# One of sixteen score blocks of a head pair copied by ScalarE and folded on GpSimd; context products in two halves of columns

## The reference

```python
attn = jnp.einsum('bhqd,bhkd->bhqk', q, k) * scale
attn = jax.nn.softmax(attn.astype(jnp.float32), axis=-1)
ctx  = jnp.einsum('bhqk,bhkd->bhqd', attn, v)
```

## Time and profile before

| what | value |
|---|---|
| runs | 3328.68 us median of 3 (3327.36 to 3344.76) |
| profiled execution | 3326.78 us, its span 3325.0 us |
| TensorE, VectorE, ScalarE, GpSimd busy | 80%, 74%, 55%, 30% of the span |
| mean granted clock of TensorE | 0.908 |
| maxima of the cuts, VectorE L708 | 1024 instructions, 1204.8 us, mean 1219 ns |
| Exp, ScalarE L693 | 2048 instructions, 1064.6 us, mean 602 ns |
| context, TensorE L632 | 4096 instructions, 547.2 us |
| scores, TensorE L645 and L619 | 2048 each, 622.6 and 526.4 us |
| GpSimd waiting for the pair's maximum (L541) | 914.6 us |

### The profile page before, as it was taken

The page is one execution under the profiler, slowest core; times in us unless marked ns, Lnnn a source line. Parts: engine busy times, 40 slices in busy tenths (PEclk is TensorE's granted clock), DMA queues, the critical chain, the costliest instruction groups (busy, mean ns, idle before and its releaser), DMA issues. The chain is left out here.

```text
span 3325.0 us, 42836 instructions
## 1 busy us (share of the span) xinstructions
PE 2664.8 (80%) x12693; PEld 959.3 (29%) x12693; DVE 2465.1 (74%) x2953; ACT 1815.3 (55%) x3157; POOL 1006.7 (30%) x1271
## 2 busy tenths in 40 slices
PE   6799999985578689999998419677777777997776
PEld 3122222222256312222221218322232232332222
DVE  6999999964245499999994532679999975447468
ACT  3488888883133358888888105355555531224423
POOL 4222222210555322222220046136777740000000
PEclk9799999997889879999999659878999998998788
DMA  4111111106333301111110411201000000000000
GB/s 122 38 26 28 24 23 23 23 15 150 49 87 105 104 18 25 24 27 25 24 23 11 145 43 53 69 19 41 13 7 13 7 0 0 0 0 12 0 0 25
DMA packets 161305, 120.15 MB, mean 36 GB/s; under 512 B 65325, under 2 KB 138925, under 8 KB 160928
## 3 DMA queue, kind: packets, MB, share of 16 engines
q1 hardware_dynamic: 123232, 75.34, 9.1%
q0 software_dynamic: 36800, 39.15, 4.3%
q10 hardware_dynamic: 1152, 4.19, 0.4%
HBM read 68.60 MB, written 49.89 MB: 36 GB/s over the span
## 5 line engine op out<-in xcount | busy, mean ns | idle before, releaser
L708 DVE TENSOR_REDUCE a_att_mx<-a_att_s 128x2 f32<-128x1024 f32 x1024 | 1204.8, 1219 | 62.0 <-PE a_att_s L619 49.7
L693 ACT ACTIVATE a_att_pt<-a_att_st 128x512 f32<-128x512 f32 x2048 | 1064.6, 602 | 232.4 <-PE a_att_st L645 231.8
L645 PE MATMUL a_att_st<-a_qst,a_kst 50*128 50x512 bf16 x2048 | 622.6, 385 | 62.9 <-ACT a_att_pt L693 51.5
L619 PE MATMUL a_att_s<-a_kst,a_qst 48*128 48x512 bf16 x2048 | 526.4, 399 | 64.4 <-DVE a_att_mx L708 32.9
L632 PE MATMUL a_att_av<-a_att_pt,a_att_vst 128*32 128x512 f32 x4096 | 547.2, 607 | 0.0
L645 PEld LDWEIGHTS a_att_st<-a_qst,a_kst 50*128 50x128 bf16 x2048 | 158.9, 94 | 726.5 <-ACT a_att_pt L693 668.1
L2286 POOL TENSOR_TENSOR g_xn<-m2s_hs,m2s_cb 128x1024 f32<-128x1024 f32 x128 | 300.8, 2354 | 119.0 <-DVE m2s_hs L2253 73.1
L2253 DVE TENSOR_TENSOR_SCAN m2s_hs<-m2s_da,m2s_bps 128x1024 f32<-128x1024 f32 x128 | 292.7, 2287 | 4.4
L541 POOL CAST a_att_mt_in<-a_att_nmax 128x16 bf16<-128x16 f32 x64 | 12.6, 198 | 914.6 <-DVE a_att_nmax L716 914.6
L2169 PE MATMUL m2s_yps<-g_xn,g_ident 128*128 128x512 f32 x512 | 242.8, 597 | 0.9
L2225 ACT COPY m2s_cb<-m2s_cps 128x1024 f32<-128x1024 f32 x128 | 129.5, 1012 | 183.9 <-POOL g_xn L2286 182.4
(11 more groups left out here) (487 smaller groups left out, 3742.6 us busy)
## 6 DMA issues: line engine op xcount, KB each, us to landing
a_qst<-a_qstk POOLq DMA_DIRECT2D x124, 64.0 KB, 2.3
a_kst<-a_kstk POOLq DMA_DIRECT2D x124, 64.0 KB, 2.4
f_xs<-f_sent SPq DMA_DIRECT2D x20, 396.0 KB, 3.7
a_qstk<-a_qkv_part SPq DMA_DIRECT2D x16, 384.0 KB, 3.0
f_sent<-f0r_zero SPq DMA_DIRECT2D x1, 5148.0 KB, 22.0
a_kstk<-a_qkv_part SPq DMA_DIRECT2D x32, 128.0 KB
a_kstk<-a_qkv_part SPq DMA_DIRECT2D x16, 256.0 KB
a_num<-a_att_oev SPq DMA_DIRECT2D x256, 16.0 KB
```

Of the source, the lines that this page charges most:

```text
L619: mm = pe.matmul(s1[:, cut % 2, h, :], qst[u][64 * h:64 * h + SPECIAL, qt * P:(qt + 1) * P], kst[u][64 * h:64 * h + SPECIAL, kh * CH:(kh + ...
L645: pe.matmul(st[:, e % 3, :], kst[u][64 * h:64 * h + STACK, kt * P:(kt + 1) * P], qst[u][64 * h:64 * h + STACK, half * CH:(half + 1) * CH], ...
L693: act.activation(pt[:, e % 16, :], st[:, e % 3, :], ACT.Exp, scale=scale).then_inc(exp_done, 1)
L708: dve.tensor_reduce(mx[:, par, 2 * cut:2 * cut + 2], s1[:, cut % 2, :, :], AX.X, ALU.max).then_inc(s1_used, 1)
```

## The change

Cut 7 of each pair is no longer reduced by VectorE. ScalarE copies it from PSUM to SBUF (`move`, before the Exp of unit 16), GpSimd folds it in four levels from 512 to 32 columns a head (`halve_moved`: max(a, b) as (a - b) clamped from below at 0, plus b, twelve instructions), and VectorE takes the maximum of what is left before the maximum over the pair, which now also waits for that. TensorE's cut 9, which uses the same PSUM buffer, waits for ScalarE's copy. The context block of a step is cut in two halves of 256 columns, except for the first and the last of a pair, and TensorE's order becomes two units, a cut, half a context block, twice a step.

```diff
+        moved = g.area[:, 4608:4608 + 2 * CH].rearrange("p (h t) -> p h t", t=CH)
+        UNITS, CUTS, OFF = 32, 16, 7
...
+                def halve_moved(n):
+                    pool.wait_ge(s1_moved, n + 1)
+                    for k in range(LEVELS):
+                        wide = CH >> (k + 1)
+                        low, high = moved[:, :, 0:wide], moved[:, :, wide:2 * wide]
+                        if k:
+                            pool.wait_ge(pool_step, 3 * LEVELS * n + 3 * k)
+                        pool.tensor_tensor(low, low, high, ALU.subtract).then_inc(pool_step, 1)
+                        pool.wait_ge(pool_step, 3 * LEVELS * n + 3 * k + 1)
+                        pool.tensor_scalar(low, low, 3.0e38, 0.0, ALU.min, ALU.max).then_inc(pool_step, 1)
+                        pool.wait_ge(pool_step, 3 * LEVELS * n + 3 * k + 2)
+                        pool.tensor_tensor(low, low, high, ALU.add).then_inc(pool_step, 1)
...
                 for b in range(1, BATCH):
                     for hp in range(PAIRS):
                         split_max(PAIRS * b + hp - 2)
                         fetch(b, hp, PAIRS * b + hp - 3)
+                        halve_moved(PAIRS * b + hp - 1)
...
-                    if not (isinstance(n, int) and n == 0 and cut < 2):
-                        pe.wait_ge(s1_used, CUTS * n + cut - 1)
+                    if cut == OFF + 2:
+                        pe.wait_ge(s1_moved, n + 1)
+                    elif not (isinstance(n, int) and n == 0 and cut < 2):
+                        pe.wait_ge(s1_used, OWN * n + (own(cut - 2) + 1 if cut >= 2 else cut - 1))
...
-                def weigh(n, u, kt):
+                def weigh(n, u, kt, part):
...
+                    if kt in (0, 7) and part == 1:
+                        return
+                    at = slice(part * CH // 2, (part + 1) * CH // 2) if 0 < kt < 7 else slice(0, CH)
...
-                        scores(n, u, kt, (0, 1), before)
-                        cut(0)
-                        scores(n, u, kt, (2,), before)
-                        if kt >= 2:
-                            weigh(n, u, kt - 2)
-                        elif before:
-                            weigh(n - 1, (u + 3) % 4, kt + 6)
-                        scores(n, u, kt, (3,), before)
-                        cut(1)
+                        for half in range(2):
+                            scores(n, u, kt, (2 * half, 2 * half + 1), before)
+                            cut(half)
+                            if kt >= 2:
+                                weigh(n, u, kt - 2, half)
+                            elif before:
+                                weigh(n - 1, (u + 3) % 4, kt + 6, half)
...
+                def move(n):
+                    act.wait_ge(s1_ready, CUTS * n + OFF + 1)
+                    if not (isinstance(n, int) and n == 0):
+                        act.wait_ge(moved_used, n)
+                    act.copy(moved[:, :, :], s1[:, OFF % 2, :, :]).then_inc(s1_moved, 1)
...
                     for e in range(UNITS):
+                        if e == 2 * OFF + 2 and first:
+                            move(4 * m + u + 2)
...
                     for cut in range(lo, hi):
+                        if cut == OFF:
+                            continue
...
-                    dve.wait_ge(s1_used, CUTS * (n + 1))
+                    dve.wait_ge(pool_step, 3 * LEVELS * (n + 1))
+                    dve.tensor_reduce(mx[:, par, 2 * OFF:2 * OFF + 2], moved[:, :, 0:CH >> LEVELS], AX.X,
+                                      ALU.max).then_inc(moved_used, 1)
+                    dve.wait_ge(s1_used, OWN * (n + 1))
+                    dve.wait_ge(moved_used, n + 1)
```

More of the change, by code:

```diff
@@ L515, in attention_stage @@
         av_ready, evac = s.sem("av_ready"), s.sem("evac")
-        UNITS, CUTS = 32, 16
+        s1_moved, pool_step, moved_used = s.sem("s1_moved"), s.sem("pool_step"), s.sem("moved_used")
+        LEVELS = 4
+        moved = g.area[:, 4608:4608 + 2 * CH].rearrange("p (h t) -> p h t", t=CH)
+        UNITS, CUTS, OFF = 32, 16, 7
+        OWN = CUTS - 1
+        own = lambda cut: cut - (cut > OFF)
         with nc.Block() as block:
@@ L558, in _ @@
                     values(0, hp)
+                halve_moved(0)
                 split_max(0)
+                halve_moved(1)
                 split_max(1)
                 fetch(0, 3, None)
+                halve_moved(2)
                 for hp in range(4, PAIRS):
@@ L621, in first_cut @@
                     mm.then_inc(s1_ready, 1)
-                def weigh(n, u, kt):
-                    if kt == 0:
+                def weigh(n, u, kt, part):
+                    if kt == 0 and part == 0:
                         pe.wait_ge(vcopied, n + 1)
@@ L631, in weigh @@
                             gr = 2 * h + half
-                            mm = pe.matmul(av[32 * gr:32 * gr + 32, :], vst[u][:, kt, h, :],
-                                           pt[:, 4 * (kt % 4) + 2 * half + h, :], start=kt == 0, stop=kt == 7)
+                            mm = pe.matmul(av[32 * gr:32 * gr + 32, at], vst[u][:, kt, h, :],
+                                           pt[:, 4 * (kt % 4) + 2 * half + h, at], start=kt == 0, stop=kt == 7)
                     if kt == 7:
@@ L676, in _ @@
                     pair(NPAIR // 4 - 1, u, u < 2, True)
-                weigh(NPAIR - 1, 3, 6)
-                weigh(NPAIR - 1, 3, 7)
+                weigh(NPAIR - 1, 3, 6, 0)
+                weigh(NPAIR - 1, 3, 6, 1)
+                weigh(NPAIR - 1, 3, 7, 0)
+                weigh(NPAIR - 1, 3, 7, 1)
             @block.scalar
@@ L686, in sums, with pair @@
                     act.copy(oev[:, u % 2, :], av[:, :]).then_inc(evac, 1)
-                def pair(m, u, before):
+                def move(n):
[3 more added lines that the diff above has]
+                    act.copy(moved[:, :, :], s1[:, OFF % 2, :, :]).then_inc(s1_moved, 1)
+                def pair(m, u, before, first=True):
                     for e in range(UNITS):
+                        if e == 2 * OFF + 2 and first:
+                            move(4 * m + u + 2)
                         if e == 7 and before:
@@ L695, in _ @@
                 act.activation(warm[:, :], g.eps[:, :], ACT.Exp).then_inc(table, 1)
+                move(0)
+                move(1)
                 for u in range(4):
                     pair(0, u, u > 0)
-                with act.Fori(1, NPAIR // 4) as m:
+                with act.Fori(1, NPAIR // 4 - 1) as m:
                     for u in range(4):
                         pair(m, u, True)
+                for u in range(4):
+                    pair(NPAIR // 4 - 1, u, True, u < 2)
                 sums(NPAIR // 4 - 1, 3)
```

2 lines of the change are left out of this document (added).

## The result

| | kernel before | kernel after |
|---|---|---|
| median of 20 runs (lowest to highest) | 3328.07 us (3323.76 to 3355.52) | 3344.79 us (3333.91 to 3364.41) |
| profiled execution, its span | 3326.78, 3325.0 us | 3347.47, 3345.8 us |
| last context copy of layer 0, of layer 1 | 756.17, 1823.15 us | 778.00, 1840.29 us |

The changed kernel takes 1.0033 of the time before (95% interval 1.0017 to 1.0049): 11 us slower by this ratio, 17 by the two medians. That is little, at or under what I had called measurable for a single comparison, but on the other side of zero from the forecast of 3298. It lies inside the range of 3252 to 3350.

What follows compares the result with a forecast made beforehand. A loop between TensorE and ScalarE, not VectorE, was taken as the bound. Gains of 21 us in pairs with cuts and 11 at layer ends, less 1 at starts, gave 31: likeliest 3298 us, range 3252 to 3350.

Steps and rivals of the forecast that it cites:

- The sum of the pair: TensorE's queue from first cut to next pair's first cut: 19.37 us against 19.72, 21 us gained over 60 pairs.
- the start: Start of a layer: 1 us lost waiting for the first fold, which starts when GpSimd has done its fetches.
- the ends: Last two pairs of a layer, without cuts: 16.6 and 14.1 us, 5.4 gained a layer, 11 in all.
- plain half steps: TensorE's two scores, one cut, half a context block without extra waits: 0.22 + 0.32 + 0.58 = 1.12 us each.
- the old period: Pair before the change: eight steps of 2.39 us, 19.12, plus context copy 0.59 on ScalarE, 19.71 against 19.72 measured.
- Half a context block: Context product of 256 columns on TensorE holds it for 0.58 us, against 1.00 for a whole block.
- Rival C: Context halves cost more than half, over 0.61 us each; with 0.70 the kernel takes 3370 us; chance 15%.
- The copied block: Cut 7 moved to ScalarE: VectorE's floor falls to 17.42 us a pair, the copy adds 0.49 to the chain.
- idle 0.94 before maximum 8 and 0.63 before maximum 9: VectorE's waits around the removed maximum: about 1.0 and 0.6 to 0.7 us, so the removal buys nothing.
- The fold: GpSimd's twelve instructions take 7.8 to 8.8 us, hidden in an 11 us window before VectorE asks for the result.
- Rivals B and E: B: VectorE bounds again, pair 18.4, 3240 us, 14%. E: GpSimd's fold late, 12 us or more, 3358 us, 3%.
- three signs of being wrong: Half W over 0.61 us; VectorE waiting for GpSimd at the small maximum; idle before maxima 8 and 9 under 1.1.

Runs made afterwards that it cites:

- the split alone: Kernel before with context product in halves and TensorE's new order; VectorE reduces all 16 cuts, no copy, no fold: 3297.38 us, 0.991 of before.
- the split without maximum 7: Kernel before with context halves and new order, no copy or fold, VectorE's maximum of cut 7 left out altogether: 3296.13 us, 0.9897.
- the copied block alone: Kernel after with whole context blocks in TensorE's old order, so only the copy and the fold: 3362.93 us, 1.0113.
- the rotation: Kernel after with score buffers taken in turn over the pair's border, unit e of pair u in buffer (e + 2u) mod 3: 3327.98 us, 0.9998.
- split and rotated: Kernel before with context halves, new order and score buffers in turn over the pair's border, no copy or fold, TensorE's loop kept: 3284.39 us, 0.9863.
- halves side by side: Kernel before in its old order, each inner context block as sixteen instructions of 256 columns, not eight of 512: 3400.62 us against 3361.09, 1.0113.
- before, written out: Kernel before with TensorE's loop of four pairs a pass as straight code, nothing else changed: 3319.25 us, 0.9978.
- after, written out: Kernel after with TensorE's loop of four pairs a pass as straight code, other engines unchanged: 3318.87 us, 0.9975.
- split and rotated, written out: Kernel before with context halves, new order, score buffers in turn over the border and TensorE's loop as straight code: 3248.68 us, 0.9758.

## Why the prediction was wrong

Two steps of the prediction failed. The sum of the pair held every unit to the Exp three units back, and at the border unit 1 waits for the one two back: 0.35 us a pair, 21 of the 31 us forecast. And TensorE's jump back was put at nothing, in the sum and in the rivals: it cost 23.7 us, which is what turned a gain into a loss. The remainders of other terms (the start, the ends) are of 2 us each.

*The rhythm, step by step.* TensorE through the border of a pair in the kernel after (its cuts, and where a wait shows):

```profile
303.30 0.64 PE L662 MATMUL a_att_av<-a_att_pt,a_att_vst 128*32 128x256 f32 x8
...
303.87 0.84 PE L675 MATMUL a_att_st<-a_qst,a_kst 50*128 50x512 bf16 x2
...
304.41 0.51 PE L646 MATMUL a_att_s<-a_kst,a_qst 48*128 48x512 bf16 x2
...
305.65 0.38 PE L646 MATMUL a_att_s<-a_kst,a_qst 48*128 48x512 bf16 x2
...
306.76 0.38 PE L646 MATMUL a_att_s<-a_kst,a_qst 48*128 48x512 bf16 x2
```

Units 0 and 1 start at 303.87 and take 0.84 for two where every other couple takes 0.39, since unit 1 waits for the Exp two units back. The cuts start at 304.41 (C0), 305.65, 306.76 (C2), and the rest of the pair at 308.30, 309.23, 310.91, 311.84, 313.09 (C7), 315.91 (C9), 317.16 (C10) and 324.13 (the next C0):

| from, to | forecast | measured |
|---|---|---|
| C10 to C0' | 6.72 | 6.97 |
| C0 to C2 | 2.24 | 2.35 |
| C2 to C3 | 1.54 | 1.54 |
| C3 to C4, C4 to C5 | 0.85, 1.76 | 0.93, 1.68 |
| C5 to C6, C6 to C7 | 0.85, 1.34 | 0.93, 1.25 |
| C7 to C9, C9 to C10 | 2.73, 1.34 | 2.82, 1.25 |
| sum | 19.37 | 19.72 |

All that lies between C2 and C10 comes to 10.40 against 10.41. The whole miss of 0.35 is in the two terms that I wrote down as plain half steps, the border: +0.25 and +0.11 (a border wait of 0.45, less 0.01 for each plain half, which takes 1.11 and not 1.12). That is the first step that failed. I had "unit e waits for the Exp of unit e-3" for every unit, when the number of the buffer restarts with the pair.

*Why the old period seemed to prove the model.* It came out to 0.01 because two terms shared one number. Starts of the context blocks in the kernel before, around the context copy and around the border, with the wait of unit 1:

```profile
304.76 1.06 PE L632 MATMUL a_att_av<-a_att_pt,a_att_vst 128*32 128x512 f32 x8
307.43 1.06 PE L632 MATMUL a_att_av<-a_att_pt,a_att_vst 128*32 128x512 f32 x8
...
319.38 1.06 PE L632 MATMUL a_att_av<-a_att_pt,a_att_vst 128*32 128x512 f32 x8
...
321.45 0.39 PE L645 MATMUL a_att_st<-a_qst,a_kst 50*128 50x512 bf16 x1 [0.47 <-ACT a_att_pt L693]
...
322.08 1.06 PE L632 MATMUL a_att_av<-a_att_pt,a_att_vst 128*32 128x512 f32 x8
```

A step of 2.39 takes 2.67 where the copy stands (+0.28) and 2.70 at the border (+0.31): 19.12 + 0.28 + 0.31 = 19.71. I had put 0.59, the copy's whole length, on the copy. Right in sum, wrong in parts, and in the new order the two parts went different ways: the copy's hides (C4 to C5 was even shorter than forecast), the border's grows to 0.45.

*The split.* Half a context block occupies 0.57 (303.30 to 303.87; forecast 0.58), a plain half step 1.11. Rival C, the dear half, is excluded by that. What spoke for a price was the page "TensorEngine Tiling (Array Packing)" of the Trainium skill, Key Properties: a change of the tiling mode drains the array. The traces agree as far as they show a price of the change, 0.14 us a step (1.14 for two halves apart, 1.00 for them side by side). Six steps of a pair pay it, 0.84 us, and the pair of the split alone is shorter all the same; a drain itself stands in no row.

*The copied block.* It costs 0.75 us a pair in the new order: 18.97 without it, 19.72 with it. I had 0.49 (C7 to C9 against two plain halves, now 2.82 against 2.22, 0.60) and nothing for what follows: cut 9's second product is late too, so C9 to C10 is 1.25 in place of 1.11. Here I had the term but no consequence of it, since 1.34 stood in that line in either case. That the pair without the copy came near its forecast (18.97 against 18.88) is luck: the border was missing from it, and the 1.34 was too much in it by about as much; with the border gone as well the pair is 18.52. VectorE, ScalarE and GpSimd around it, in the kernel after:

```profile
307.23 0.21 DVE L758 TENSOR_REDUCE a_att_mx<-g_area 128x2 f32<-128x64 f32 x1
...
307.79 0.20 POOL L546 CAST a_att_mt_in<-a_att_nmax 128x16 bf16<-128x16 f32 x1 [4.15 <-DVE a_att_nmax L764]
...
314.25 1.02 ACT L722 COPY g_area<-a_att_s 128x1024 f32<-128x1024 f32 x1
...
314.62 1.23 DVE L752 TENSOR_REDUCE a_att_mx<-a_att_s 128x2 f32<-128x1024 f32 x1 [0.94 <-PE a_att_s L646]
...
315.36 1.26 POOL L559 TENSOR_TENSOR g_area<-g_area 128x512 f32<-128x512 f32 x1 [2.32 <-ACT g_area L722]
...
316.47 5.75 DVE L752 TENSOR_REDUCE a_att_mx<-a_att_s 128x2 f32<-128x1024 f32 x5 [0.63 <-PE a_att_s L646]
...
323.05 0.32 POOL L563 TENSOR_TENSOR g_area<-g_area 128x64 f32<-128x64 f32 x1
```

The rest of this part held. VectorE is idle 0.94 before maximum 8 and 0.63 before maximum 9 (forecast 1.0 and 0.6 to 0.7), so that the removed maximum buys nothing, which the split without maximum 7 showed by itself. The fold takes 8.0 us (315.36 to 323.37; forecast 7.8 to 8.8), and GpSimd then waits 4.15 for VectorE: hidden. Rivals B and E are out. None of the three signs of being wrong that I had named came up either (half a block over 0.61, VectorE waiting for GpSimd, idle time under 1.1): they watched the parts that held, and only the period, 19.72 in place of 19.4, and the last pair but one, 17.25 in place of 16.6, gave the miss away.

*The ends.* The last pair but one takes 17.25, with a border in it too (forecast 16.6), the last 14.33 (14.1): 4.5 us gained a layer, forecast 5.4. Layer 0 starts 3.0 us late, forecast 1, and layer 1 only 0.2. In layer 0 the clock goes with it: it stays at 1.2 GHz through this window (kernel after, then before), where the old order was at full clock nearly throughout.

```profile
131.00:138.30 7.30, 7.30 (x44) 1.27 (x40) 3.35 (x4) 5.13 (x9) 2.79 (x5) 0.50 0.16 41
```

```profile
131.00:138.30 7.30, 7.28 (x50) 1.70 (x48) 6.48 (x6) 6.18 (x12) 0.85 (x3) 0.97 0.13 29
```

The split alone starts 4.5 us late (152.75), the copied block alone 2.4 (150.56), but the split without maximum 7 only 0.8 (149.00). What of this is cause and what effect I did not take apart.

*The stalls*, 23.7 us, were in no term and in no rival, and are the second step that failed. Of the 31 us forecast, 21 were lost to the border (60 x 0.35) and 24 to stalls, 2 more at the start, 2 at the ends: 18 us slower, with the 3.7 behind the stages 22, where the two profiled executions differ by 20.7. By the ratios of the runs, the change without stalls is worth 8 us (0.9975), and the rotation another 12 in the loop (1.0033 to 0.9998).

What a stall is, the loading queue shows. Its packets over the whole execution, beside the stalls counted in the same trace:

| kernels | TensorE's loop | stalls | packets of q8 |
|---|---|---|---|
| before; the copied block alone | 128 matmuls a pair | 0 | 58 |
| after; the split alone; after, rotated | 176 | 3 | 94 |
| split and rotated; split without maximum 7 | 176 | 4 | 103 |
| halves side by side | 176 | 5 | 112 |
| before, written out | none | 0 | 97 |
| after, written out; split and rotated, written out | none | 0 | 121 |

In the loop kernels with 176 matmuls a pair each stall goes with nine packets. By time they stand where the stalls do: in each of the 22 stalled passes of these six traces nine packets start, the first 4.3 to 4.9 us before TensorE goes on, and the other eight jumps back of layer 0 and the 30 of layer 1 have none. So TensorE stands still while instructions of its loop are loaded again. With the code written out the same queue brings a packet every 10 to 18 us, and TensorE stands still nowhere in the stage.

What brings it on is shown less fully. The stalls are there in six kernels (after, the split alone, the two rotated ones in the loop, the one without maximum 7, the halves side by side) whose loop body has 176 matmuls a pair on TensorE (64 of scores and cuts, 112 of context; the halves side by side the same), with and without the copy and the fold, in either order, at paces of 18.5 to 19.8 us a pair, and always at one of the five jumps back. They are not there with 128 matmuls a pair in the loop (before, the copied block alone), and not with 176 written out. So it takes the jump and the split. That it is the length of the body, and not something else of products of 256 columns, is the likely reading, as it is instructions that are loaded, but no run lengthened or shortened the body in another way, with two pairs a pass for instance. It also stays open why the body is loaded again at some jumps and not at others, and why never in layer 1, which runs the same order in a loop of the same length.

## What to carry to other kernels

When a model reproduces the old period from one term that is as long as an instruction, look at each place by itself: the same sum may hide two waits, and the change will treat them differently. A number of buffers that does not divide the number of units of a loop body makes the first units of each pass wait for an Exp one unit nearer; numbering on through the passes gave 0.45 us a pair here. An edit that makes the body of a TensorE loop longer is to be tested once with the loop written out, and the queue that loads instructions is to be read by windows and not only in total. Work taken from an engine that is kept waiting by others is worth nothing, while the copy that takes it away stands in the chain.

## What the runs showed of the hardware

Context products of 256 columns in four column groups cost no more than half of one of 512: sixteen in 1.00 us against eight in 1.00.

With a loop body of 704 matmuls (4 pairs of 176) TensorE stood still at three to five of the five jumps back of one stage and at none of the next, for 2.9 to 4.5 us and soon after for 0.7 to 2.1; with the clock lower behind it (in the one shown for some 8 us) a stall cost 6 to 9 us. At each of the 22 the queue of instructions loaded nine packets, 0.15 MB, and at the other jumps none. A body of 512 had no stall, and written-out code none, though it loads all the time.

GpSimd's operations on two float32 operands in SBUF took 1.27, 0.73, 0.46 and 0.32 us for 512, 256, 128 and 64 elements a partition, and the clamp 0.61, 0.40, 0.29 and 0.24: about 0.18 us each plus 2.1 and 0.83 ns an element.
